# Raw offset copies on ScalarE, GELU in eight blocks and token-mask sums on TensorE in a four-stage convolution kernel

## What is computed

```python
x = x + L0(_gn(x))   # whitening: one 128 x 128 matrix for all pixels
x = x + L1(_gn(x))   # deformable convolution
x = x + L2(_gn(x))   # attention in 7 x 7 windows, then between the window tokens
x = x + L3(_gn(x))   # masked image, ReLU, 3 x 3 convolution

def L1(x):                       # per pixel: 16 groups of channels, 9 taps
    xproj = x @ in_w + in_b
    x1 = gelu(layernorm(depthwise3x3(x)) * ln_g + ln_b)
    offset = x1 @ off_w + off_b                  # 16 * 9 * 2 per pixel
    mask = softmax(x1 @ mask_w + mask_b, taps)   # 16 * 9 per pixel
    return sum_over_taps(mask * bilinear(xproj, tap + offset)) @ out_w + out_b

def L3(x):
    mu_x = clip(round(sum(ix * x) / sum(x)));  mu_y = ...   # from row and column sums, per channel
    m = max(1 - (|posX - mu_x| + |posY - mu_y|) * mask_weight, -1)
    return conv3x3(relu(x * m)) + bias
```

## Time and profile before

| | |
|---|---|
| runs | 10,800.67, 10,726.73 and 10,787.02 us, median 10,787.02 |
| profiled execution | 10,794.42 us, span 10,792.5 us |
| mean granted TensorE clock | 0.865 of full speed |
| busy share of the span | PE 81%, DVE 69%, ACT 34%, POOL 2% |
| the mask sums' first instruction (L1896) | 16 times, first start 1376.7, last 10721.2 us |

### The profile page before, as it was taken

One profiled execution on the slowest core, in us unless ns is written; L12 is line 12 of the kernel. 1 busy time (PEld: TensorE's weight loads), 2 busy tenths in 40 slices (PEclk: granted clock), 3 DMA queues, 4 the chain that ended last, 5 costly groups with the idle time before them and its releaser, 6 DMA issues.

```text
span 10792.5 us, 288961 instructions
## 1 busy us (share of the span) xinstructions
PE 8769.2 (81%) x124030; PEld 4760.4 (44%) x124030; DVE 7397.8 (69%) x9080; ACT 3634.9 (34%) x5874; POOL 191.5 (2%) x254
## 2 busy tenths in 40 slices
PE   5468888887888888788888878888887888888786
PEld 5324444353444435344343544434354443535344
DVE  2477676768666776776677677677867767786763
ACT  0024333242333424333342433324243332424332
POOL 0000000000000000000000000000000000000000
...
GB/s 105 6 12 35 43 21 40 35 34 37 40 42 19 42 36 35 38 39 40 22 42 34 36 39 27 45 27 44 29 41 39 24 45 29 46 28 42 40 21 51
DMA packets 230314, 391.72 MB, mean 36 GB/s; under 512 B 25200, under 2 KB 166480, under 8 KB 221776
## 3 DMA queue, kind: packets, MB, share of 16 engines
...
## 4 chain that ended last, share of the span: by engine, by line
PE 56%; DVE 26%; issue 11%; ACT 5%; DMA 1%; DVEq 0%; SPq 0%; ACTq 0%; POOL 0%; POOLq 0%
PE ps L880 9%; PE ps L683 7%; PE ps L748 7%; PE ps L781 4%; PE ps L756 4%; DVE arena L1685 3%; PE ps L797 3%; PE ps L980 3%; DVE arena L1662 3%; DVE arena L1668 3%; DVE arena L1745 3%; PE ps L970 3%; PE ps L705 2%; PE ps L770 2%; DVE arena L1782 1%
## 5 line engine op out<-in xcount | busy, mean ns | idle before, releaser
L880 PE MATMUL ps<-arena,ident 64*64 64x512 f32 x5600 | 1946.0, 734 | 797.8 <-DVE arena L1685 768.7
L882 PE MATMUL ps<-arena,ident 48*64 48x512 f32 x5600 | 1951.3, 735 | 0.9 <-issue 0.6
L1685 DVE TENSOR_TENSOR arena<-arena 112x2560 f32<-112x2560 f32 x560 | 1573.8, 2817 | 50.4 <-PE ps L882 50.4
L880 PEld LDWEIGHTS ps<-arena,ident 64*64 64x64 f32 x5600 | 531.4, 158 | 1903.4 <-issue 1891.3
L748 PE MATMUL ps<-arena,wqk 128*128 128x400 f32 x2048 | 961.3, 594 | 166.4 <-DVE arena L1791 119.0
L1776 DVE COPY arena<-ps 128x400 f32<-128x400 f32 x512 | 293.3, 573 | 856.5 <-PE ps L748 855.3
L683 PE MATMUL ps<-vp,convw 128*128 128x448 f32 x2016 | 819.9, 550 | 23.6 <-ACT vp L1293 23.6
L1668 DVE TENSOR_TENSOR arena<-arena 112x576 f32<-112x576 f32 x1008 | 764.1, 758 | 34.9
L781 PE MATMUL ps<-ident,arena 128*128 128x128 f32 x4096 | 619.7, 300 | 204.0 <-ACT arena L1221 56.6
L797 PE MATMUL ps<-arena 64*64 64x33 f32 x32768 | 674.0, 234 | 96.0 <-issue 58.0
L756 PE MATMUL ps<-wv,arena 128*64 128x256 f32 x4096 | 647.1, 441 | 107.0 <-ACT arena L1164 95.7
...
## 6 DMA issues: line engine op xcount, KB each, us to landing
...
arena<-windows_out SPq DMA_DIRECT2D x224, 256.0 KB, 4.1
arena<-windows_out SPq DMA_DIRECT2D x224, 192.0 KB, 3.4
...
out_x<-xb SPq DMA_DIRECT2D x112, 224.0 KB, 2.0
```

What stands on the lines that cost most here:

```text
L880: nc.tensor.matmul(ps[half, 3, :], ident[0:SLOT, 0:SLOT], prod[0:SLOT, ring(c, dy), dx, :], start=(s < 2), stop=(s >= TAPS - 2), skip_grou ...
L882: mm = nc.tensor.matmul(ps[half, 4, :], ident[SLOT:PT, SLOT:], prod[SLOT:PT, ring(c, dy), dx, :], start=(s < 2), stop=(s >= TAPS - 2), ski ...
L1685: V.tensor_tensor(prod[0:PT, ring(c, dy), :, :].rearrange("p k (n e) -> p k n e", e=CG), taps.to_broadcast([PT, SHIFTS, N64, CG]), for_tap ...
```

## The change

1. **Offsets.** ACT copies each half of the projection's result from PSUM to SBUF in one instruction (`copy_offsets`, three values of 9 taps, 2 pixels and 16 groups: 864 elements on 112 partitions). PE waits for this copy alone before it uses the banks again. The three readings of the offsets, and DVE's subtraction of the maximum, now take the copy, the latter in one pass over all four pixels (`shift_mask`, at (c, 1)) in place of two passes from PSUM at (c, 0) and (c, 2); the exponential is one instruction at (c, 2). A separate buffer `terms` takes `by_row`'s products.
2. **Projections.** Half 0 of tile c + 2 moves from (c, 3) to (c, 4), half 1 of tile c + 1 from behind the taps of (c, 1) to ahead of the taps of (c, 0).
3. **GELU.** Eight blocks of 392 elements by groups of tile rows, two at the end of each of steps 21 to 24, in place of seven of 448 at the end of step 24.
4. **Token mask.** ACT writes the normalised image in two parts. At q = 40 PE adds up the image in PSUM with the identity as weights, seven matmuls by blocks of rows into bank 1 and seven by blocks of columns into bank 0; DVE reduces each bank's 448 elements to 56 sums at q = 42, in place of the five instructions on the image at q 41 and 42.

```diff
-DVE_PRE, DVE_MAIN, DVE_BLK, DVE_END = 6 + 8 * DW_BLOCKS, 112, 69, 46
+DVE_PRE, DVE_MAIN, DVE_BLK, DVE_END = 6 + 8 * DW_BLOCKS, 105, 69, 42
...
-                    pe.wait_ge(of_h.sem, of_h.at(n, s - OFF_AT + 1))
-                    pe.wait_ge(of_s.sem, of_s.at(n, s - OFF_AT + 1))
+                    pe.wait_ge(of_c.sem, of_c.at(n, s - OFF_AT + 1))
...
             def project(n, c, half):
-                pe.wait_ge(y1_g.sem, y1_g.at(n, c + 1))
-                pe.wait_ge(of_h.sem, of_h.at(n, 2 * c + half))
-                pe.wait_ge(of_s.sem, of_s.at(n, 2 * c + half))
+                pe.wait_ge(y1_g.sem, y1_g.at(n))
+                pe.wait_ge(of_c.sem, of_c.at(n, 2 * c + half))
                 project_bias(0, 6)
...
+                elif q == GN_Q + 3:
+                    for half in range(2):
+                        pe.wait_ge(v3_s.sem, v3_s.at(i, half + 1))
+                        for k in range(4 * half, min(4 * half + 4, CHUNKS)):
+                            nc.tensor.matmul(ps[:, 1, 0:CH], ident, vp_in[:, k * ROWS:(k + 1) * ROWS, :],
+                                             start=(k == 0), stop=(k == CHUNKS - 1))
+                    for k in range(CHUNKS):
+                        mm = nc.tensor.matmul(ps[:, 0, 0:CH], ident, vp_in[:, :, k * ROWS:(k + 1) * ROWS],
+                                              start=(k == 0), stop=(k == CHUNKS - 1))
+                    mm.then_inc(vs_p.sem, 1)
...
+                        if dy == 0 and c + 1 < TR:
+                            project(n, c + 1, 1)
                         if s < TR * SHIFTS - 1:
                             sum_taps(n, c, dy)
-                        if dy == 1 and c + 1 < TR:
-                            project(n, c + 1, 1)
...
-                        elif dy == 3 and c + 2 < TR:
+                        elif dy == 4 and c + 2 < TR:
                             project(n, c + 2, 0)
...
-                    read_offsets(n, 0, s - 1 - OFF_AT)
+                    copy_offsets(n, 0, s - 1 - OFF_AT)
+                elif s == OFF_AT + 3:
+                    exp_mask(n, 0)
...
-                    exp_mask(n, 0, s - 1 - OFF_AT)
                     hats(n, 0, s - 1 - OFF_AT)
-                elif s == BC_AT + TWO:
-                    act.wait_ge(ln_y.sem, ln_y.at(n))
-                    for y in range(TR):
-                        nc.scalar.activation(y1g[:, y].rearrange("c t (a b) -> c t a b", a=TY), x1c_tile[:, y], ACT.Gelu,
-                                             bias=lnb, scale=lng).then_inc(y1_g.sem, 1)
+                elif BC_AT < s <= BC_AT + TWO:
+                    act.wait_ge(ln_y.sem, ln_y.at(n, min(2 * (s - BC_AT), TR)))
+                    for a in range(2 * (s - 1 - BC_AT), 2 * (s - BC_AT)):
+                        nc.scalar.activation(y1g[:, :, :, a * TX:(a + 1) * TX].rearrange("c y t b -> c y b t"),
+                                             x1c[:, a * TR * W:(a + 1) * TR * W].rearrange("c (y b t) -> c y b t", y=TR, t=T4),
+                                             ACT.Gelu, bias=lnb, scale=lng).then_inc(y1_g.sem, 1)
...
+            def copy_offsets(n, c, half):
+
+                act.wait_ge(of_p.sem, of_p.at(n, 2 * c + half + 1))
+                if c:
+                    act.wait_ge(rw_s.sem, rw_s.at(n, c))
+                else:
                     act.wait_ge(y1_g.sem, y1_g.at(n))
+                nc.scalar.activation(by_half(offsets_of(c)[0][0:PT, :], half),
+                                     ps[0:PT, off_bank(c):off_bank(c) + 2, 0:OFFS].rearrange("p t (q g) -> p q t g", g=G1),
+                                     ACT.Copy).then_inc(of_c.sem, 1)
...
+            def hats(n, c, half):
+                h, offs = hats_of(n, c, half), by_half(offsets_of(c)[0][0:PT, 0:2 * HN], half)
+                act.wait_ge(of_c.sem, of_c.at(n, 2 * c + half + 1))
...
-                    nc.scalar.activation(vp_in, xb_yx, ACT.Identity, bias=sm[:, 29:30], scale=sm[:, 28:29]
-                                         ).then_inc(v3_s.sem, 1)
+                    for rows in (slice(0, 4 * ROWS), slice(4 * ROWS, H)):
+                        nc.scalar.activation(vp_in[:, rows, :], xb_yx[:, rows, :], ACT.Identity, bias=sm[:, 29:30],
+                                             scale=sm[:, 28:29]).then_inc(v3_s.sem, 1)
...
+                copy_offsets(n, 1, 0)
...
+                        if ahead and dy == 0:
+                            copy_offsets(n, c + 1, 1)
+                        elif ahead and dy == 2:
+                            exp_mask(n, c + 1)
                         if i is not None:
                             after_windows(i, 2 * s)
-                        if c + 1 < TR and dy in (0, 2):
-                            exp_mask(n, c + 1, dy // 2)
-                            read_offsets(n, c + 1, dy // 2)
-                            hats(n, c + 1, dy // 2)
+                        if ahead and dy < 2:
+                            hats(n, c + 1, dy)
+                        elif c + 2 < TR and dy == 4:
+                            copy_offsets(n, c + 2, 0)
...
+            def shift_mask(n, c):
+
+                logits = logits_of(c)
+                dve.wait_ge(of_c.sem, of_c.at(n, 2 * c + 2))
+                ownm.step(V.tensor_reduce(mx1[0:PT, :], logits.rearrange("p (q n) -> p n q", q=P9), AX.X, ALU.max))
+                V.tensor_tensor(logits.rearrange(by_tap, q=P9), logits.rearrange(by_tap, q=P9), per_pixel(mx1), ALU.subtract
+                                ).then_inc(ms_s.sem, 1)
...
-                elif q == GN_Q + 4:
-                    dve.wait_ge(v3_s.sem, v3_s.at(i))
-                    owne.mark(V.tensor_reduce(rsum[:, 0:W], vp_in, AX.X, ALU.add))
                 elif q == GN_Q + 5:
-                    owne.step(V.tensor_tensor(mk[:, 0:28], vp_in[:, 0:28], vp_in[:, 28:56], ALU.add))
-                    owne.step(V.tensor_tensor(mk[:, 28:42], mk[:, 0:14], mk[:, 14:28], ALU.add))
-                    owne.step(V.tensor_tensor(mk[:, 42:49], mk[:, 28:35], mk[:, 35:42], ALU.add))
-                    owne.step(V.tensor_reduce(rsum[:, W:], mk[:, 42:49].rearrange("c h w -> c w h"), AX.X, ALU.add))
+                    dve.wait_ge(vs_p.sem, vs_p.at(i))
+                    V.tensor_reduce(rsum[:, 0:W], ps[:, 0, 0:CH].rearrange("c (h a) -> c h a", h=H), AX.X, ALU.add)
+                    owne.step(V.tensor_reduce(rsum[:, W:], ps[:, 1, 0:CH].rearrange("c (a w) -> c w a", w=W), AX.X, ALU.add))
...
-                        if ahead and dy in (0, 2):
-                            shift_mask(n, c + 1, dy // 2)
+                        if ahead and dy == 1:
+                            shift_mask(n, c + 1)
```

55 lines of the change are left out of this document (19 added, 36 removed).

## The result

The changed kernel took 10812.6 us (median of 20 runs, 10773.5 to 10848.4), the kernel before 10763.6 us (20 runs, 10719.5 to 10811.0): ratio 1.0038, 95% interval 1.0025 to 1.0052. The forecast was 10,836 us and no measurable change; the change is small but clear of the noise, and a second comparison gave 1.005 (1.0026 to 1.0073). The profiled execution has a span of 10812.2 us.

What follows compares the result with a forecast made beforehand. No engine is full; PE and DVE alternately bound a turn. Terms -9.2 + 3 + 7 + 2.1 = +2.9 us a turn, times 15 = +44, last image +5: 10,843, less 7.4 for the median, 10,836 us; range 10,600 to 11,005.

Steps and rivals of the forecast that it cites:

- First image: First image's sampling, ahead of the first turn: the prediction had no term for it.
- The last image: Last image, without sampling: the mask's sums on PE cost 11.3 + 1.3 - 7.7 = +5 us, once.
- GELU and first offsets: Windows phase, ahead of tile 0: GELU blocks and offset copies save 9.2 us a turn, between -12.5 and -6.
- its three terms: Windows phase, per turn: earlier ACT copy and PE -5.7 us, higher PE clock -3, extra table loads +2.5 (0 to 5).
- the offsets' copies: Steps 26 and 27: one ACT copy replaces PE's wait for three readings, 1.5 us a step, 3 us saved.
- Projections, tiles 0 to 3: Two projections side by side: +3.9 us on tile 1, -1 for tiles 2 and 3; sum +3, between +1 and +5.
- Token mask: Tile 4: DVE waits for PE's sums, so its work from the mask on comes 7 us later, between 4.5 and 12.
- Tile 5: Tile 5 on: projection (6, 0) now uncovered, 2.6 - 0.5 = +2.1 us, carried to the turn's end.
- End of the turn: Last convolution piece to the next turn: the prediction had no term for it.
- The low clock: Rival, q = 40 in tile 4: products run at low clock, a turn loses 13.4 us, 10,998 us; chance 0.28.
- DVE's load is what counts: Rival, tile 4: unloading DVE gains 18 us a turn, 10,517 us, or some 10,650 with sums even; chance 0.21.
- Table loads on the path: Rival, steps 21 to 24: ACT cannot hide 7.7 us of loads, turn +8.1 us, 10,914 us; chance 0.08.

Runs made afterwards that it cites:

- 3: Changed kernel with GELU in one burst of seven by tile again, copies of offsets kept; ratio 1.0111 to the kernel before.
- 4: Changed kernel with GELU in two groups of four blocks instead of four groups of two; ratio 1.0102 to the kernel before.
- 9: Changed kernel with projections at their places of before, copies kept, mask's maximum and exponential one step later; ratio 0.9961 to the kernel before.
- 5: Changed kernel with the token mask's sums on DVE again, image in one part, no identity products; ratio 0.9963 to the kernel before.
- 6: Changed kernel with the mask's sums on DVE again and ACT's image ahead of its second copy of offsets; ratio 0.9929 to the kernel before.
- 1: Changed kernel with DVE's far flag back in dy = 2 of tile 6 instead of dy = 4; ratio 0.9956 to the kernel before.
- 7: Changed kernel with identity products ahead of second projection and taps of (4, 0), image ahead of second copy; ratio 1.0003 to the kernel before.
- 8: Kernel before with only the mask's sums moved to PE, 14 identity products behind the taps of (4, 0); ratio 1.0030 to the kernel before.
- 10: Changed kernel with projections at their old places, far flag early, mask's column sums on PE, rows on DVE; ratio 0.9827, 10585.7 us.

## Why the prediction was right, and where its terms were off

The time was right, 0.2% high, and the turn that was foretold (636) is the one of the profile. The forecast was 49 us over the kernel before (44 + 5), and the medians differ by 49.0; what it is high by is its base, the median of three runs (10,787.0) for that of twenty (10,763.6). That is partly luck: of the turn's terms two were too small, one too large and one missing, and a term outside the turns was missing too.

- **First image** (not in the sum, -21.9 once). The working counts turns and a last image. The first image's sampling, where DVE waited 28.7 us for the projections, stands ahead of the first turn; a gain there makes up for half of the 44 us. Worked back from the medians, with what lies outside the turns as profiled, a turn got (49.0 + 21.9 - 1.8) / 15 = 4.6 us longer (an estimate) for 2.6 in the profiles; the profiled execution of the kernel before was 31 us above its median, 2.1 us a turn. By this estimate the 2.9 foretold was 1.7 too low, and the two misses cancelled in the total. The last image was put at +5; all that lies behind the last turn grew by 1.8 us.

- **GELU and first offsets** (-9.2 forecast, -14.4 measured, beyond its own bound of -12.5). The named rows came as foretold: blocks of 0.95 us in 1.91, loads of 1.28 us, PE's wait at L756 0.19 us, strided writes no dearer. Burst against blocks measured 7.9 where its three terms (GELU 5.7, clock 3, table loads 2.5 against them) give 6.2, so 1.7 of the 5.2 us are theirs; the clock, counted at 3, rose from 0.74 to 0.86 over the stretch, and of the 2.5 for the table loads nothing could be seen (3, 4). The larger miss is the offsets' copies: counted at 3, about what PE's direct wait fell by (3.5 us a turn), and worth 6.5 with all that followed from them, which no run takes apart. (ACT is "the least loaded engine" only beside PE and DVE; POOL is busy 2%.) A load ends at 4277.07 + 1.28 = 4278.35 and GELU starts at 4278.37, so again no drain shows, against the estimate that the Trainium skill would give (ScalarE: Activation LUTs, What ACT_TABLE_LOAD costs).
- **Projections, tiles 0 to 3** (+3, +3.6). By the tiles' own starts tile 1 lost 3.5 (3.9 forecast), tiles 2 and 3 gained 0.9 (1), tile 0 lost 1.0 (none). Only tile 1 bears the mechanism out: its loss goes when the projections go back (9), while the sum of the four tiles stays.
- **Token mask** (+7, +4.9). DVE's wait is 11.6 us for 13 foretold. In the turn shown the first projection ran at full clock (2.6 us for 4.9). The chain that the forecast laid out, taps and then products, is the one in the trace, and "ACT's image in two parts has time enough behind its second copy" holds for it. What the chain did not say is that the sums' way back to DVE would gain only 1.2 us (5), because the image, 2.9 us later than it could be, comes to stand in their place (6).
- **Tile 5** (+2.1, +4.1). The placement is worth 3.2 here and 1.6 more in tile 6 (9).
- **End of the turn** (0, +4.1). The missed step. The working follows the moved projections through PE, ACT and DVE, but not the far flag, a wait of DVE that SP's load stands behind. A delay of a 0.14 us instruction by two steps cost 5.3 us a turn (1), more than putting the mask's sums back on DVE gained (5).
- **Rivals.** The low clock did not come in the changed kernel (0.88 from 4530 to 4586) but did in 7. "DVE's load is what counts" is wrong for the turn as a whole: taking 6.5 us of sums off DVE made tile 4 longer (8). It came true in the first image, and once PE's part ran beside DVE's (10). Table loads on the path: 3 and 4, with fewer of them, are slower.
